# An attention and routed-expert kernel: first loads reordered, GpSimd splits every fourth weight unit

## The reference

```python
# x: 8 x 512 x 512, ctx_1024: 8 x 120 x 512, all f32
x = x + xattn(ctx_1024, ctx_1024, layernorm(x), Wk, Wq, Wv, Wo, bq, bv, bo)   # one head, D = 512
x = x + ffn(layernorm(x), Wg, bg, W1, b1, W2, b2)                             # 8 experts, 512 -> 512 -> 512
# ffn: expert = argmax(softmax(x @ Wg + bg)); out = gelu(x @ W1[expert] + b1[expert]) @ W2[expert] + b2[expert]
```

## Time and profile before

| | |
|---|---|
| median of 3 runs | 462.82 us (461.86 to 467.15) |
| the profiled execution's own time | 464.17 us |
| its span in the profile | 462.5 us |
| PE busy | 414.7 us (90%) |
| DVE, ACT, POOL busy | 249.7, 211.4, 184.5 us |
| first transpose of a tile of x on PE | 114.18 us |
| mean granted clock of PE | 0.971 |

### The profile page before, as it was taken

How to read it: one execution, slowest core, us unless ns; L and a number is a source line. 1 busy time by engine, 2 the same in 40 slices (tenths; PEclk the granted TensorE clock), 3 DMA queues, 4 the chain that set the end, 5 groups by cost and what they waited for, 6 DMA issues and landing times.

```text
span 462.5 us, 8003 instructions
## 1 busy us (share of the span) xinstructions
PE 414.7 (90%) x2083; PEld 223.8 (48%) x2084; DVE 249.7 (54%) x615; ACT 211.4 (46%) x427; POOL 184.5 (40%) x233
## 2 busy tenths in 40 slices
PE   6858999998999989897897999989989999999980
PEld 2445665564766767664343333434434444444430
DVE  0245999777367776886437244444444554544420
ACT  1233346745788878786522653232324333333210
POOL 8000000600115544447454337465546565665420
PEclk9979999999999998998899999999999999999996
DMA  8999986840836567545677969898989988889620
GB/s 243 345 314 383 377 330 227 300 155 4 298 93 184 165 230 241 155 148 161 151 193 186 203 153 167 188 184 172 192 178 208 184 200 182 199 195 205 118 47 0
DMA packets 116007, 90.88 MB, mean 197 GB/s; under 512 B 86642, under 2 KB 86654, under 8 KB 115975
## 3 DMA queue, kind: packets, MB, share of 16 engines
q1 hardware_dynamic: 108735, 70.55, 60.8%
q0 software_dynamic: 6400, 19.65, 12.7%
q10 hardware_dynamic: 840, 0.29, 0.4%
HBM read 50.37 MB, written 21.06 MB: 154 GB/s over the span
## 4 chain that ended last, share of the span: by engine, by line
PE 70%; DMA 15%; DVE 6%; issue 3%; ACT 1%; SPq 1%; POOLq 0%; POOL 0%; DVEq 0%; ACTq 0%
PE bank L1428 23%; PE bank L1431 11%; DMA ey_bias_split_then_geluT<-work 6%; PE bank L1360 5%; PE bank L1378 5%; DMA work<-in_ctx 5%; PE bank L1340 5%; PE bank L1290 4%; PE bank L1268 3%; PE bank L1353 3%; DMA out_x<-keys_values_then_rows_b 3%; PE bank L1250 2%; PE bank L1371 1%; DMA expert_weights<-key_bias_then_xn 1%; PE bank L1419 1%
## 5 line engine op out<-in xcount | busy, mean ns | idle before, releaser
L1428 PE MATMUL bank<-expert_weights 128*128 x312 | 75.5, 386 | 7.5 <-DMA expert_weights<-key_bias_then_xn 4.2
L1428 PE MATMUL bank<-expert_weights,ey_bias_split_then_geluT 128*128 x312 | 74.3, 381 | 5.5 <-DMA ey_bias_split_then_geluT<-work 5.5
L643 POOL DMA_INDIRECT out_x<-keys_values_then_rows_b x39 | 44.5, 1141 | 81.7 <-DVE keys_values_then_rows_b L1129 77.3
L823 ACT ACTIVATE work<-work 128x512 f32<-128x512 f32 x31 | 19.5, 630 | 112.0 <-DVE work L1184 112.0
L1129 DVE SCALAR_TENSOR_TENSOR keys_values_then_rows_b<-bank,keys_values_then_rows_b 128x512 f32<-128x512 f32 x39 | 27.0, 691 | 74.2 <-PE bank L1431 74.2
L1428 PEld LDWEIGHTS bank<-expert_weights 128*128 128x128 f16 x312 | 30.3, 99 | 46.5 <-issue 13.9
L699 ACT ACTIVATE expert_weights<-expert_weights 128x512 f16<-128x512 f32 x64 | 38.8, 626 | 29.6 <-DVE expert_weights L921 28.8
L1428 PEld LDWEIGHTS bank<-expert_weights,ey_bias_split_then_geluT 128*128 128x128 f16 x312 | 30.0, 98 | 43.9 <-issue 11.8
L603 POOL DMA_INDIRECT routed_rows<-work,slot_index x32 | 33.0, 1031 | 39.1 <-DVE slot_index L1015 31.6
L921 DVE SCALAR_TENSOR_TENSOR expert_weights<-expert_weights 128x512 f16<-128x512 f32 x64 | 41.9, 692 | 1.1 <-ACT expert_weights L699 0.6
L1431 PE MATMUL bank<-expert_weights 128*128 x156 | 40.9, 386 | 0.0
(11 more groups left out here) (186 smaller groups left out, 648.9 us busy)
## 6 DMA issues: line engine op xcount, KB each, us to landing
expert_weights<-in_L_ffn_W SPq DMA_DIRECT2D x14, 1024.0 KB, 9.5
keys_values_then_rows_b<-routed_rows SPq DMA_DIRECT2D x39, 258.0 KB, 2.9
expert_weights<-in_x SPq DMA_DIRECT2D x16, 512.0 KB, 8.9
expert_weights<-in_x SPq DMA_DIRECT2D x24, 256.0 KB, 3.2
routed_rows<-keys_values_then_rows_b POOLq DMA_DIRECT2D x9, 258.0 KB, 9.3
keys_values_then_rows_b<-in_x SPq DMA_DIRECT2D x8, 256.0 KB, 4.1
expert_weights<-in_L_ffn_W SPq DMA_DIRECT2D x8, 256.0 KB, 3.3
work<-in_ctx SPq DMA_DIRECT2D x1, 1920.0 KB, 22.7
```

Source lines behind the costliest of these rows:

```text
L643: pool.indirect_dma_start(out_rows, ids_of, rrow[t.buf][:, 0:D], None, bounds_check=T - 1, oob_is_err=False).then_inc(out_sent[t.buf], 16)
L1428: mm(o, a[:, c, :], w_split[:, bass.ds(first + (2 * c + h) * D, D)], start=(c == 0 and h == 0 and not begun), stop=False)
```

## The change

The edits belong together:

- SP's first loads come in the order Wk and Wq, Wo, the context in two halves of four batches (each with a semaphore of its own), Wv, then x groups 0 to 3. The transposed Wo moves from `work`, where the context lies, to the place of the values of batches 0 to 3, and PE transposes Wo ahead of the context.
- DVE reads no x group ahead of the context's low parts; all 16 follow, and the low halves of units are spread anew (`at_group`).
- POOL alone splits units 3, 7, 11, ... 47, in three operations: the source times 64 in place (f32), its copy to f16 (high), and source minus high (low, f16). ACT and DVE leave these units out; who needs unit n - 2 split waits for POOL's semaphore where that unit is POOL's.
- POOL's queue becomes: units 3 to 31, the scalars of x, the nine padding writes (before: in front of all), units 35 to 47.
- ACT issues the broadcasts of bo and bg behind its context copies, normalises tile 0 before the last job of the preparation, and does expert 5's high halves after that.

```diff
+POOL_UNITS = tuple(range(3, 48, 4))
...
-        woT = work[:, 0:C * D].rearrange("p (c n) -> p c n", c=C)
+        woT = kvb[:, 0:C, 1, :]
...
+        def shared(n):
+            return n - sum(1 for m in POOL_UNITS if m < n)
+        def split_by(eng, n):
+            if n in POOL_UNITS:
+                eng.wait_ge(pool_split, POOL_UNITS.index(n) + 1)
+            else:
+                eng.wait_ge(low_done, shared(n) + 1)
...
+        J_WOT = job("act", C)
         J_CTX = job("both", B)
-        J_WOT = job("act", C)
...  (SP)
-            load_group(0)
-            sp.dma_start(ctx_nat[0:K, :, :], ctx_in.rearrange("b k d -> k b d")).then_inc(ld["ctx"], 16)
-            load_group(1)
             sp.dma_start(wo_sb, chunked(Wo)).then_inc(ld["wo"], 16)
-            load_group(2)
+            for h in range(2):
+                sp.dma_start(ctx_nat[0:K, 4 * h:4 * h + 4, :],
+                             ctx_in[4 * h:4 * h + 4].rearrange("b k d -> k b d")).then_inc(ctx_half[h], 16)
             sp.dma_start(wv_sb, chunked(Wv)).then_inc(ld["wv"], 16)
-            load_group(3)
+            for n in range(NM):
+                load_group(n)
...  (POOL)
-            for e in range(E + 1):
-                pool.dma_start(routed[SPAN * e:SPAN * e + P, :], pad_row).then_inc(pad_out, 16)
+            def split(n):
+                pool.wait_ge(w_early[n // NW], 32)
+                split_by(pool, n - GAP)
+                src = wall[:, (n + GAP) * D:(n + GAP + 1) * D]
+                hi, lo = (w_split[:, n * 2 * D + D * h:n * 2 * D + D * (h + 1)] for h in range(2))
+                link(nc.gpsimd.tensor_scalar(src, src, WSCALE, 1.0, ALU.mult, ALU.mult))
+                link(nc.gpsimd.tensor_scalar(hi, src, 1.0, 0.0, ALU.mult, ALU.add))
+                nc.gpsimd.tensor_tensor(lo, src, hi, ALU.subtract).then_inc(pool_split, 1)
+
+            for n in POOL_UNITS:
+                if n < (NEARLY - 2) * NW:
+                    split(n)
             pool.wait_ge(stats1, NT)
...
             nc.gpsimd.tensor_tensor(std1[:, :], ve1[:, :], rstd1[:, :], ALU.mult).then_inc(scal1, 1)
+
+            for e in range(E + 1):
+                pool.dma_start(routed[SPAN * e:SPAN * e + P, :], pad_row).then_inc(pad_out, 16)
+
+            for n in POOL_UNITS:
+                if n >= (NEARLY - 2) * NW:
+                    split(n)
...  (ACT)
-            act.dma_start(bo_bc, bo.partition_broadcast(P)).then_inc(ld["bo"], 16)
-            act.dma_start(bg_bc[:, :], bg.partition_broadcast(P)).then_inc(ld["bg"], 16)
...
-                need(act, low_done, n - GAP + 1)
+                if n >= GAP:
+                    split_by(act, n - GAP)
...
-                    high(2 * NW + 2 * m + q)
+                    if 2 * NW + 2 * m + q not in POOL_UNITS:
+                        high(2 * NW + 2 * m + q)
...
             act.wait_ge(scal1, 3)
+            step(-1, U - 1, -1)
+            high_of(NEARLY - 1)
             act.wait_ge(pre_mm, NJOBS)
-            for k in range(-1, NT):
+            for k in range(0, NT):
...  (DVE)
-            moments_of_x(0)
             for k in range(C):
                 n = J_KQ + k
                 low_part(n, [kq[:, h, k, :] for h in range(2)], bank[n % 8][:, :], WSCALE)
-                if k == 1:
-                    moments_of_x(1)
...
-                dve.wait_ge(high_done, n + 1)
+                dve.wait_ge(high_done, shared(n) + 1)
...
-            at_group = [0] * 6 + [2] * 4 + [4] * 2 + [2] * 3 + [NW + 2]
+            early_units = [n for n in range((NEARLY - 2) * NW) if n not in POOL_UNITS]
+            at_group = [0] * 4 + [2] * 12
             n_low = 0
-            for n in range(2, NT // M):
+            for n in range(0, NT // M):
                 moments_of_x(n)
-                if n == 5:
+                if n == 3:
...
-                if 6 <= n < 6 + C - 1:
-                    k = n - 5
+                if 4 <= n < 4 + C - 1:
+                    k = n - 3
                     low_part(J_OV + k, [ov[:, h, k, :] for h in range(2)], bank[(J_OV + k) % 8][:, :], WSCALE)
                 for m in range(at_group[n]):
-                    low(n_low + m)
+                    low(early_units[n_low + m])
...
                 for m in range(2):
-                    low((NEARLY - 2) * NW + 2 * b + m)
+                    if (NEARLY - 2) * NW + 2 * b + m not in POOL_UNITS:
+                        low((NEARLY - 2) * NW + 2 * b + m)
...  (PE: the transposes of Wo stand ahead of those of the context; in these)
+                if b % 4 == 0:
+                    pe.wait_ge(ctx_half[b // 4], 16)
```

More of the change, by code:

```diff
@@ L704, in _ @@
                 copy(n, kq[:, 0, k, :], bank[n % 8][:, :], WSCALE)
+            for k in range(C):
+                n = J_WOT + k
+                copy(n, woT[:, k, :], bank[n % 8][:, :])
             for b in range(B):
@@ L1228, in _ @@
             last.then_inc(pre_mm, 1)
-            pe.wait_ge(ld["ctx"], 16)
-            for b in range(B):
-                n = J_CTX + b
-                free(n)
-                for c in range(C):
-                    last = nc.tensor.transpose(bank[n % 8][:, K * c:K * (c + 1)], ctx_nat[0:K, b, P * c:P * (c + 1)],
-                                               ident[0:K, 0:K])
-                last.then_inc(pre_mm, 1)
             pe.wait_ge(ld["wo"], 16)
@@ L1245, in _ @@
                                                ident[:, :])
+                last.then_inc(pre_mm, 1)
+            for b in range(B):
+                n = J_CTX + b
+                free(n)
+                if b % 4 == 0:
+                    pe.wait_ge(ctx_half[b // 4], 16)
+                for c in range(C):
+                    last = nc.tensor.transpose(bank[n % 8][:, K * c:K * (c + 1)], ctx_nat[0:K, b, P * c:P * (c + 1)],
+                                               ident[0:K, 0:K])
                 last.then_inc(pre_mm, 1)
```

30 lines of the change are left out of this document (18 added, 12 removed).

## The result

The changed kernel takes 480.53 us (median of 6 runs, 479.05 to 483.97) where the kernel before takes 464.77 in the same series: ratio 1.033 [1.029, 1.038], 3.3% slower. 475.4 was forecast for the profiled execution and 474.0 for the median. The order of events came out as forecast, and so did the moment at which the loop over x tiles starts; the total is 6.5 us higher on the median. Of these, 1.9 us lie in the kernel before, whose median is 464.77 us in this series and was 462.82 when the forecast was made: the change costs 15.8 us, 11.2 were forecast, so 4.6 us were missed.

A forecast was written before the change was run, and what follows sets the result against it. TensorE was taken to set the preparation's end, other lists only just covered. Last value copy +10.5 us, normalisation already done saving 0.3, clock +1: sum +11.2, so 475.4 us profiled, 474.0 on the median, range 466 to 481.

The forecast's parts named there:

- Load order: Front of the preparation: first product with Wv starts at 28.3 instead of 37.26, 8.9 us earlier.
- DVE's loop: VectorE's 16 x groups: waits added, group 11 ends at 69.5, statistics complete at 86.1 against 81.7 before.
- The port: GpSimd's splits beside VectorE's low halves: they exclude one another; VectorE waits 1.9 us at units 9 and 17, 0.3 at 12.
- The rival without hindrance: GpSimd and VectorE don't hinder each other, the pad wait stays: +4 to +7 us, 467 to 470; chance 0.22.
- The padding writes: GpSimd's queue: scalars end at 98.4, writes issued until 103.4, landed 4 us later at 107.5; VectorE's value copies wait for them.
- The value copies: Eight copies and twelve low halves behind the pads, 4.74 us a round: last copy at 124.4 against 113.86, +10.5 us.
- The clock: TensorE's 9.5 us standstill before the first x tile lowers its clock: at most 1.8 us lost, partly hidden, +1.
- Loops: Tile and expert loops after the preparation: untouched by the change.

The follow-up runs named there:

- e2: Changed kernel without GpSimd's units and with the padding writes in front (load order alone); ratio 0.991 to the kernel before.
- e6: Changed kernel without GpSimd's units, padding writes behind VectorE's second low half; ratio 0.991 to the kernel before.
- e9: Changed kernel without GpSimd's units, padding writes left late, behind the scalars; ratio 1.0005 to the kernel before.
- e8: e6 plus GpSimd doing a split's three operations seven times on a constant, result unused, nothing waiting for it; ratio 0.999 to the kernel before.
- e7: Changed kernel with units 3 to 31 given back to ScalarE and VectorE, GpSimd keeping 35 to 47; ratio 1.011 to the kernel before.
- e3: Changed kernel with units 35 to 47 given back to ScalarE and VectorE, padding writes still late; ratio 1.023 to the kernel before.
- e5: Changed kernel with the padding writes directly behind GpSimd's unit 3; ratio 1.012 to the kernel before.
- e1: Changed kernel with the padding writes back in front of GpSimd's queue; ratio 1.017 to the kernel before.
- e12: Same kernel as e11, timed again in more rounds; ratio 0.990 to the kernel before, median 460.15 against 464.37 us.
- e4: Changed kernel with 62 unused 128x512 products on TensorE behind the last value product; ratio 1.036 to the kernel before.
- e10: Kernel before, its load order and padding writes in front kept, with GpSimd's twelve units alone added; ratio 1.017 to the kernel before.
- e11: e6 with the row weights' low half moved ahead of group 15's low halves; ratio 0.985 [0.976, 0.994] to the kernel before.

## Why the prediction was right, step by step

**Load order: right.** Forecast 28.3 for the first Wv product, measured 28.91; ACT's and DVE's context copies, 24.7 forecast, start at 25.18. e2 and e6 show what it is worth without POOL's units and late writes: 4 us of the 8.9, as DVE's loop comes next.

**DVE's loop: right, to 0.8 us, and part of that is luck.** Statistics forecast at 86.1, measured 85.31; expert 3's wait forecast 3.5, measured 3.89; PE's wait for the row weights forecast to end at 87.6, measured 87.21. What follows was taken over from the kernel before at 27.2 us, to end at 114.8; it took 29.3 and ended at 116.5, as the 24 products behind the wait ran slow. The late padding writes hid that. The parts were mixed: group 11 ended at 68.30 (forecast 69.5). Where POOL's unit does not interfere, a group with its two low halves takes 2.81 us; where it does, 3.76 to 3.81, so 0.96 for each unit in POOL's pace, where 1.9 had been put down at units 9 and 17. The key to e9's 75.65 against 85.31 is 0.9 from the start, 3.9 for expert 3's wait (e9's list leaves unit 24 to the last group and never meets it), and five times 0.96.

**The port: the mechanism right, its size over.** POOL's operations alone take 0.62, 0.62 and 1.15 us, not 0.76, 0.76 and 1.26. Beside low halves they read 0.92 and 1.65:

```profile
57.31 0.62 POOL L587 TENSOR_SCALAR expert_weights<-expert_weights 128x512 f16<-128x512 f32 x1
58.01 1.66 POOL L588 TENSOR_TENSOR expert_weights<-expert_weights 128x512 f16<-128x512 f32 x1
```
```profile
57.96 0.69 DVE L960 SCALAR_TENSOR_TENSOR expert_weights<-expert_weights 128x512 f16<-128x512 f32 x1
59.35 0.87 DVE L960 SCALAR_TENSOR_TENSOR expert_weights<-expert_weights 128x512 f16<-128x512 f32 x1 [0.69 <-ACT expert_weights L730]
```

The low half came 0.05 us first and kept its 0.69; POOL lost the 0.51. At 53.23 in e8 they started together and both ended late. This is the case that the earlier trace rows had left open, the two-input operation against a series, and it agrees with the rule of the Trainium skill (SBUF — State Buffer, Who interferes with whom) that the two exclude one another. The power again does not. In e8 it takes 5.46 us, as in the changed kernel, where DVE does next to nothing beside it, and the two low halves that lie inside it take what they always take:

```profile
90.89 5.46 POOL L606 TENSOR_TENSOR rstd_x<-var_eps_x,minus_half 128x32 f32<-128x32 f32 x1
```
```profile
93.59 1.28 DVE L967 SCALAR_TENSOR_TENSOR expert_weights<-expert_weights 128x512 f16<-128x512 f32 x2
```

The rival without hindrance forecast statistics at 83.5, pads out at 104.6 and 467 to 470 us; it falls by e8.

**The padding writes: right by two errors that cancel.** Scalars forecast to end at 98.4, measured 95.97, since POOL's operations are shorter; the landing was put 4 us after the last issue and took 7.7 (9.5 in e9). The sum, 107.5, came out at 108.7. The value of 4 between the bounds 1.2 and 9.3 was not supported by anything but the load left on the queue, and e7 and e9, with 9.8 and 9.5, lie outside the bounds.

**The value copies: right, again by two misses that cancel.** They began 1.2 us later than forecast, and 4.74 us a round were forecast, 4.41 measured; last copy at 124.4 forecast, 124.51 measured; start forecast 10.2 us late, measured 10.4.

**The clock: the step that was mis-sized.** +1 us was put down: half of the 3.6 us at the low clock that the earlier trace rows show, less what ACT's and DVE's share of the chain would hide. PE had clock 0.50 for 7.8 us of its loop, from 124.62 to 132.4, and little of it was hidden: its instructions there took 2.9 us more than at clock 1.00 (a tile's four transposes 1.09 us instead of 0.63), and the lag grew by 2.4. It is 2.0 in e3, 1.9 in e7 (lag 1.0 at the start, 2.9 at the fourth x tile), 2.6 in e9, and nothing in e5 (6.9, then 7.0) or e6 (-5.0, then -4.9), whose PE stood for 0.83 us ahead of the loop. Two kernels don't fit that order: e1 and e8 stood for 0.83 us too, had clock 0.50 for 3.4 us in the first tiles, and lost 1.3 and 1.4. So a long stand brought the low clock each time, and it also came without one, which stays open.

The same cost stands in a second place, for which the forecast had no term: PE's wait for the row weights. The first row is the changed kernel's, the second e2's:

```profile
87.21:91.40 4.19, 4.19 (x11) 1.39 (x12) 2.60 (x6) 0.00 (x0) 3.94 (x4) 0.50 0.98 358
```
```profile
80.68:85.71 5.03, 5.02 (x24) 2.02 (x24) 4.38 (x7) 5.03 (x11) 5.03 (x1) 1.00 0.95 357
```

In the kernel before, e2, e7, e9 and e12, where that wait is 0.5 us or none, the 24 products take 5.03 us. Behind a wait of 2.49 us (e6) to 10.77 us (e1) they take 6.71 to 7.41. In the changed kernel and in e3 and e4 the padding writes hide this; in e1, e5, e6, e8 and e10, where the products set the end, it is 1.7 to 2.4 us of the start.

**Loops: "untouched" was not quite true.** In the profiled executions the lag goes from 12.8 us at the fourth x tile to 14.3 at the last, and to 18.8 at the end of the span. The part in the x tiles is no matter of one edit: it is 0.6 to 2.1 us in nearly every kernel here (1.3 in e2, 1.7 in e6), and about 5 in e8 and e11. The part in the expert tiles is: 4.5 us here and 2.5 in e4, while e1, e2, e3, e5, e6, e8 and e10 lose none there, e7 0.3 and e9 1.0. Of the 4.5, 2.8 us are one step, at 327 us; the changed kernel's row is the first, that of before the second:

```profile
327.08 3.51 PE L1471 MATMUL bank<-expert_weights,ey_bias_split_then_geluT 128*128 x8 [2.38 <-DMA ey_bias_split_then_geluT<-work]
```
```profile
311.17 1.90 PE L1428 MATMUL bank<-expert_weights,ey_bias_split_then_geluT 128*128 x8 [1.16 <-DMA ey_bias_split_then_geluT<-work]
```

PE waits 1.2 us longer for transposed rows, and then works at clock 0.50 until 330.4, which costs 1.6. Why the rows come later there is not shown, and one profiled execution each can't show that it belongs to the change: the changed kernel's stood 2.5 us above its own median.

On the medians, the 15.8 us of the change are 10.4 at the start, 2.4 for the clock and 3.0 in the loops. Against the forecast of 11.2 the 4.6 us that were missed are 0.2, 1.4 and 3.0; what causes the last stays open. The medians of the experiments point the same way, but no more than that: the writes' late place costs 4 us without POOL units (e9 against e2 and e6) and 9.9 with them (the changed kernel against e5), where the starts differ by 3.5 and the clock adds 2.4; the 4.0 that are left are barely more than the 3.7 that the two intervals leave free.

**The sum by ratios.** Order alone -0.9%, units alone +1.7%, together (writes early) +1.2 to +1.7%, the writes' late place +2.1% with both. The first two nearly add up; the last costs more with units than without (0.9%), since units delay the scalars that it stands behind, and then pace the copies behind it.

## What to carry to other kernels

Before you move work to an idle engine, look at what is queued there behind it and who waits for that: here GpSimd had 70 us of idle time, and the first thing that it delayed was a row of transfers on which another engine's whole list stood. Work that hands a buffer from engine to engine in a ring takes the sum of its members' steps for each round (here 2.86, 0.63 and 0.69 us, and 0.23 between them), so taking four low halves from VectorE made its list 2.4 us longer. And an early gain counts only up to the next list that is full: test the edits of a bundle one by one, as the one that gained 4 us was hidden under two that lost.

## What the runs showed of the hardware

- A GpSimd operation and a two-input VectorE operation hold each other up also when they share no data and VectorE waits for no semaphore of GpSimd's: 0.85 us for a pair of low halves beside a 1.1 us TENSOR_TENSOR (e8). GpSimd's 128x512 TENSOR_SCALAR goes from 0.62 to 0.92 us, its TENSOR_TENSOR from 1.15 to 1.65. Its 5.46 us power of 128x32 does not hold up the low halves inside it (1.28 us, e8).
- It is not only two-input operations. The four copies of 128x64 f32 (L991) take 2.07 us in the changed kernel, with GpSimd's unit 31 beside them, and 0.90 in e6 and in the kernel before, where GpSimd has only operations of 128x32 by then. The first row is the changed kernel's, the second e6's:

```profile
87.08 2.07 DVE L991 COPY keys_values_then_rows_b<-gate_weights_centred 128x64 f32<-128x64 f32 x4
```
```profile
85.13 0.90 DVE L991 COPY keys_values_then_rows_b<-gate_weights_centred 128x64 f32<-128x64 f32 x4
```

- Where VectorE waits for a transfer and for a product, the profile may name either: the same 11.5 us stand under PE in the changed kernel and under the DMA in e3.
- After 8.1 us without a product TensorE had clock 0.50 for the next 7.8 us, its instructions took 2.9 us more, and 2.4 of these came back in the loop's time. After a wait of 2.49 us (e6) the next 24 products took 6.71 us instead of 5.03, with clock 0.50 until 83.4; after one of 0.47 us (e2) they took 5.03 at clock 1.00.
